# Reordering one step of a pipelined decoder: the next block's query projection between the two halves of the weighing, and FFN pieces in other places

## What is computed

```python
def attn_layer(x, Wqkv, qs, ksc, Wo):          # x: 4 x 512 x 128, 16 heads of 64
    q, k, v = split(x @ Wqkv)
    q, k = rotary(l2norm(q) * qs), rotary(l2norm(k) * ksc)
    out = local_attention(q, k, v)             # windows of 32, each looks one window back
    return out @ Wo
def ffn_layer(x, g, bln, W1, b1, W2, b2):
    xn = layernorm(x) * g + bln
    a, gate = split(xn @ W1 + b1)              # 341 + 341 columns
    return a * gelu(gate) @ W2 + b2
for i in range(6):
    x = attn_layer(shift_tokens(x), ...) + x
    x = ffn_layer(shift_tokens(x), ...) + x
```

## Time and profile before

| what | value |
|---|---|
| median of 3 runs | 2215.07 us (2211.49 to 2216.2) |
| profiled execution, its own time | 2222.9 us |
| its span, first to last instruction | 2221.1 us |
| PE matmuls busy | 2012.4 us, 91% of the span |
| DVE, ACT, POOL busy | 64%, 62%, 49% |
| mean granted PE clock | 0.983 of full speed |

### The profile page before, as it was taken

The page is one execution under the profiler, slowest core; times in us unless marked ns, Lnnn a source line. Parts: engine busy times, 40 slices in busy tenths (PEclk is TensorE's granted clock), DMA queues, the critical chain, the costliest instruction groups (busy, mean ns, idle before and its releaser), DMA issues.

```text
span 2221.1 us, 74774 instructions
## 1 busy us (share of the span) xinstructions
PE 2012.4 (91%) x32616; PEld 1183.0 (53%) x32616; DVE 1410.5 (64%) x1975; ACT 1384.2 (62%) x2029; POOL 1090.0 (49%) x709
## 2 busy tenths in 40 slices
PE   8999997789998999999999999999899998999987
PEld 5655654355555555555555555555555555555553
DVE  1454444667766776676667667766677676667753
ACT  5555554466666666766666666666666666666664
POOL 0000000576665665565656656665556555556540
PEclk9999998799999999999999999999999999999998
DMA  3000000122223222232222323222322223222220
GB/s 106 1 1 1 1 20 29 39 59 59 59 68 78 68 69 59 64 93 62 68 62 68 85 58 84 61 58 69 78 69 69 59 59 88 67 69 59 60 59 20
DMA packets 82066, 128.11 MB, mean 58 GB/s; under 512 B 17230, under 2 KB 28108, under 8 KB 81740
## 3 DMA queue, kind: packets, MB, share of 16 engines
q1 hardware_dynamic: 81740, 123.33, 21.4%
HBM read 21.55 MB, written 1.05 MB: 10 GB/s over the span
## 4 chain that ended last, share of the span: by engine, by line
PE 66%; ACT 13%; issue 11%; DVE 7%; POOL 2%; DMA 0%; ACTq 0%; POOLq 0%; DVEq 0%; SPq 0%
PE ps L617 11%; PE ps L613 11%; PE ps L639 8%; PE ps L677 7%; PE ps L670 6%; PE ps L697 4%; PE ps L426 3%; PE ps L622 3%; DVE work L1104 2%; PE ps L626 2%; ACT work L974 2%; POOL work L1421 2%; ACT work L981 2%; DVE work L1252 2%; PE ps L519 1%
## 5 line engine op out<-in xcount | busy, mean ns | idle before, releaser
L1421 POOL TENSOR_TENSOR work<-work,RS 128x1024 f32<-128x1024 f32 x192 | 365.6, 1904 | 345.8 <-ACT RS L961 342.0
L617 PEld LDWEIGHTS ps<-ident,work 128*128 128x128 f32 x3072 | 344.4, 141 | 254.5 <-issue 112.9
L617 PE MATMUL ps<-ident,work 128*128 128x128 f32 x3072 | 408.7, 276 | 68.4 <-ACT work L981 32.0
L1099 DVE TENSOR_TENSOR work<-ps,work 128x512 f32<-128x512 f32 (+1 forms) x288 | 244.6, 849 | 253.7 <-ACT work L1019 182.5
L1442 POOL TENSOR_TENSOR work<-work 128x1024 f32<-128x1024 f32 x96 | 225.8, 2352 | 149.1 <-DVE work L1104 148.9
L1427 POOL TENSOR_TENSOR work<-work,RL 128x1024 f32<-128x1024 f32 x96 | 182.8, 1904 | 141.8 <-DVE RL L1159 141.8
L1432 POOL TENSOR_TENSOR work<-work 128x1024 f32<-128x1024 f32 x96 | 226.8, 2362 | 51.0 <-DVE work L1104 51.0
L1104 DVE TENSOR_TENSOR work<-ps,work 128x512 f32<-128x512 f32 (+1 forms) x288 | 246.9, 857 | 0.0
L1144 DVE TENSOR_REDUCE SS<-work 128x16 f32<-128x1024 f32 x192 | 231.9, 1208 | 0.0
L677 PEld LDWEIGHTS ps<-work 64*32 64x32 f32 x12288 | 136.2, 105 | 166.9 <-issue 153.8
L670 PEld LDWEIGHTS ps<-KT,work 64*32 64x32 f32 x12288 | 136.6, 105 | 127.5 <-issue 125.7
(11 more groups left out here) (184 smaller groups left out, 3177.9 us busy)
## 6 DMA issues: line engine op xcount, KB each, us to landing
work<-work SPq DMA_DIRECT2D x576, 128.0 KB
work<-work SPq DMA_DIRECT2D x336, 64.0 KB
WQ<-in_wqkv SPq DMA_DIRECT2D x6, 512.0 KB, 3.6
WK<-in_wqkv SPq DMA_DIRECT2D x6, 512.0 KB, 4.1
WV<-in_wqkv SPq DMA_DIRECT2D x6, 512.0 KB, 3.5
WO<-in_wo SPq DMA_DIRECT2D x6, 512.0 KB, 3.9
work<-ZR SPq DMA_DIRECT2D x48, 64.0 KB
W<-in_w SPq DMA_DIRECT2D x6, 341.0 KB, 3.0
```

What stands on the lines that cost most here:

```text
L617: m = nc.tensor.transpose(flat(R)[:, t * 128:t * 128 + 128], src[:, t * 128:t * 128 + 128], ident[:, :])
L1099: V.tensor_tensor(h16(cos_part[:, j, cols]), h16(src), rotary_tabs[:, at:at + 64].unsqueeze(1).broadcast_to([PARTS, heads_in, 64]), ALU.mu ...
L1421: U.tensor_tensor(h16(qk_norm[:, j, :]), h16(cos_part[:, j, :]), inv_norms[:, j, :].unsqueeze(2).broadcast_to([PARTS, 16, 64]), ALU.mult). ...
```

## The change

PE: the query projection leaves the head of the step; `queries(g+1)` for the next block stands between W1 and W2, and block 0's stands before the loop. V now opens the step; Th follows it. Tk follows Th and an FFN piece. FFN pieces move: `hid(0)` before Th, `hid(1)` right behind Th, the gate of chunk 2 behind Tk, its value half behind Tq, two of the three `ffn_project` matmuls in step 1 behind S2 and the third in step 2 behind Th, three of `project_out` of step 3 behind Th, `variance` ahead of W1. ACT: squares of Q open the step, then `copy_heads` of the block weighed in the step before, then V's copy, Th's copy and the rest; the exponentials of the step's own scores stand near its end, and `invert_norms(g, 1)` last. DVE: the probability sums stand at the end of the step, `norm` ahead of `sums(1)`. POOL: the special order for step 1 goes.

PE's step after: V, [hid 0], Th, FFN piece, Tk, [gate 2], Tq, [value 2], K, S1, Tp, S2, FFN piece, W1, [project_out piece], Q of the next block, W2.

```diff
+            def queries(g):
+                pe.wait_ge(block_shifted, 2 * (g + 1))
+                pe.wait_ge(wq_loaded, 16 * (g // 16 + 1))
+                project(bank_z, w_q, 0, g % 4)
+                project(bank_z, w_q, 1, g % 4).then_inc(q_projected, 1)
...
-                if a:
-                    pe.wait_ge(block_shifted, 2 * (g + 1))
-                    pe.wait_ge(wq_loaded, 16 * (g // 16 + 1))
-                    if due(g - 2):
-                        pe.wait_ge(probs_turned_copied, g - 2)
-                    elif due(g):
-                        pe.wait_ge(q_turned_copied, g - 1)
-                    project(bank_z, w_q, 0, n)
-                    project(bank_z, w_q, 1, n).then_inc(q_projected, 1)
-                if d:
-                    pe.wait_ge(heads_copied, g - 2)
-                    turn(bank_y, heads).then_inc(heads_turned, 1)
                 if b:
                     pe.wait_ge(wv_loaded, 16 * ((g - 1) // 16 + 1))
...
+                if f is not None and n == 1:
+                    pe.wait_ge(w1_loaded, 16 * (f // 4 + 1))
+                    pe.wait_ge(ffn_input, f + 1)
+                    hid(0, bank_f)
+                if d:
+                    pe.wait_ge(heads_copied, g - 2)
+                    turn(bank_y, heads).then_inc(heads_turned, 1)
+                if f is not None and n == 0:
+                    centre(f)
+                if f is not None and n == 1:
+                    pe.wait_ge(hidden_gated, 3 * f + 1)
+                    hid(1, bank_f)
+                if f is not None and n == 2:
+                    ffn_project(f, 2, 3)
+                if fo is not None and n == 3:
+                    project_out(fo, 3, 6)
                 if b:
                     pe.wait_ge(k_normed, g)
...
+                    pe.wait_ge(gate_gelu, 3 * f + 2)
+                    hid_gate(2, bank_f)
                 if b:
                     if a:
                         pe.wait_ge(q_sin, g + 1)
...
+                if f is not None and n == 1:
+                    pe.wait_ge(hidden_gated, 3 * f + 2)
+                    hid_value(2, bank_f)
                 if a:
                     pe.wait_ge(wk_loaded, 16 * (g // 16 + 1))
...
+                if f is not None and n == 0:
+                    variance(f)
                 if f is not None and n == 1:
-                    pe.wait_ge(hidden_gated, 3 * f + 1)
-                    hid(1, bank_f)
+                    ffn_project(f, 0, 2)
...
                     weigh(0, 4)
...
+                if g + 1 < ALL_BLOCKS:
+                    if not b:
+                        pe.wait_ge(q_sin, g + 1)
+                    queries(g + 1)
                 if c:
                     weigh(4, 8).then_inc(heads_weighed, 1)
```

More of the change, by code:

```diff
@@ L751, in step @@
                     weigh(0, 4)
[L752 to L756, removed]
                 if fo is not None and n == 2:
@@ L974, in step @@
                     A(squares[:, 0, :], flat(bank_z), ACT.Square).then_inc(q_squared, 1)
+                if d:
+                    copy_heads(g - 1)
+                if f is not None and n == 1:
+                    nc.scalar.preload_act_table_set(GELU)
+                if b:
+                    act.wait_ge(values_ready, g)
+                    if due(g - 1):
+                        act.wait_ge(windows_loaded, 160 * (g - 1))
+                    A(v_rows[:, (n - 1) % 2, :], flat(bank_x), ACT.Copy).then_inc(values_copied, 1)
+                if f is not None and n == 1:
+                    gelu(f, 0, bank_f)
                 if d:
@@ L981, in step @@
                     A(heads_t[:, :, slot * 128:slot * 128 + 128], turned(bank_y), ACT.Copy).then_inc(heads_turned_copied, 1)
[L982 to L988, removed]
+                if f is not None and n == 1:
+                    gelu(f, 1, bank_f)
                 if b:
@@ L999, in step @@
                 if f is not None and n == 1:
-                    nc.scalar.preload_act_table_set(GELU)
+                    gelu(f, 2, bank_f)
                 if b:
@@ L1024, in step @@
                     A(probs_t[:, :, :], turned(bank_z), ACT.Copy).then_inc(probs_turned_copied, 1)
[L1025 to L1036, removed]
-                    inverse(f)
[L1038 to L1041, removed]
-                        copy_heads(g)
+                if f is not None and n == 0:
+                    inverse(f)
+                if b:
+                    act.wait_ge(scores_shifted, g)
+                    if due(g - 1):
+                        act.wait_ge(probs_turned, g - 1)
+                    A(probs[:, :, :, :], scores_sb[:, :, :, :], ACT.Exp).then_inc(probs_exp, 1)
+                if a:
+                    invert_norms(g, 1)
             def last_square(b):
@@ L1165, in step @@
                     rotary_cos(g, n, 0, flat(bank_z), slice(0, 1024), q_cos)
+                if f is not None and n == 1:
+                    gated(f, 0, bank_f)
+                if a:
                     if due(g):
@@ L1169, in step @@
                     sums(0, g)
+                if f is not None and n == 1:
+                    gated(f, 1, bank_f)
+                    gated(f, 2, bank_f)
                 if f is not None and n == 2:
                     update(f)
-                if f is not None and n == 1:
-                    gated(f, 0, bank_f)
                 if a:
@@ L1189, in step @@
                     V.tensor_tensor(scores_sb[:, :, :, :], by_head(bank_x), per_head(row_max[:, :]).unsqueeze(3).broadcast_to([PARTS, 8, 2, 64]), ALU.subtract).then_inc(scores_shifted, 1)
-                if f is not None and n == 1:
-                    gated(f, 1, bank_f)
+                if f is not None and n == 0:
+                    norm(f)
                 if a:
                     sums(1, g)
-                if f is not None and n == 0:
-                    norm(f)
+                if b:
+                    dve.wait_ge(probs_exp, g)
+                    V.tensor_reduce(per_head(row_sum[:, :]), probs[:, :, :, :], AX, ALU.add).then_inc(probs_sum, 1)
+                    dve.wait_ge(probs_sum, g)
+                    if due(g - 1):
+                        dve.wait_ge(probs_ready, g - 1)
+                    V.reciprocal(row_inv[:, :], row_sum[:, :]).then_inc(probs_inverse, 1)
                 if fo is not None and n == 3:
@@ L1436, in step @@
                         pool.wait_ge(block_shifted, 2 * g + 4)
-                    late = f is not None and n == 1
-                    if not late:
-                        norm_product(g, 0)
+                    norm_product(g, 0)
                     pool.wait_ge(k_cos, 2 * g + 2)
```

48 lines of the change are left out of this document (11 added, 37 removed).

## The result

The changed kernel takes **2183.96 us** (median of five runs, 2173.51 to 2189.16) against 2216.2 us for the kernel before in the same comparison (2211.49 to 2217.7): ratio **0.9861, interval 0.9841 to 0.9881**. That is 32 us less, three times the 10 us that I forecast, and inside the range of 2170 to 2242. The profiled execution of after is the fastest of the five: 2173.51 us, span 2171.7, mean granted clock 0.983. The other four have clocks of 0.975 to 0.980.

What follows compares the result with a forecast made beforehand. PE, 91% busy, was taken as the bound: 73.6 us a pass becomes 73.3 (-6 us), steps without FFN -6, tail +2, together -10: 2222.9 to 2213, or 2205 us at the median; 80% range 2170 to 2242.

Steps and rivals of the forecast that it cites:

- Instruction gaps: PE running out of instructions inside S and W: 3.0 us a pass before, 1.0 left after, W's gaps gone.
- S1, Tp, S2 is as it was, and keeps its gaps: Scores on PE: order unchanged, so S's gaps stay in steps 0, 2 and 3; part of the 1.0 us left.
- the gaps of step 0 fall into a wait anyway: Gaps in step 0 were said to cost nothing extra, falling into a wait of step 1.
- Work and waits, 71.0: PE per pass after the change: 66.7 us of work and 4.3 of waits.
- The 0.5 at Th ahead of `hid(1)`: Step 0 to 1: Th waits 0.5 us for its copy of the heads, before a 2.7 us stall at hid(1).
- The clock: Granted clock falls behind the stall at hid(1) in some 85% of passes, 1.5 us each: 1.3 us a pass, bounds 0 and 1.7.
- The eight steps without FFN: 131.6 us before, 16.4 a step; near 15.0 a step after plus 0.4 for the clock, gaining 6 us in all.
- The tail: Steps 97 and 98: hid 1 waits for gelu 0 with little beside it, costing 2 us.
- Instruction gaps stay: Rival: PE's gaps follow bytes used, not spacing, so all 3.0 us a pass remain: 2249 us; chance 0.12.
- Slower by ACT's queue: Rival: ACT's queue ahead of hid(1) in step 1 runs 1.2 us later than counted: 2231 us; chance 0.19.
- No fall: Rival: the stall at hid(1) is there but the clock holds, 29 us less: 2176 us; chance 0.17.
- the order in the text forbids it: Said against the rival that half the hid(1) stall is hidden, 64 us less: 2141 us; chance 0.07.

Runs made afterwards that it cites:

- a_both_s: Changed kernel with sums(1) ahead of norm, GELU load and gelu 0 early, and one project_out matmul between S1 and Tp in steps 2 and 3: 2111.48 us, ratio 0.9574.
- a_q_end: Changed kernel with Q of the next block behind W2 instead of between W1 and W2: 2216.38 us, ratio 1.0008 to the kernel before.
- a_norm_late: Changed kernel with sums(1) ahead of norm on DVE in step 0: 2132.18 us, ratio 0.9626 to the kernel before.
- a_gelu_first: Changed kernel with heads copy, GELU load and gelu 0 first on ACT in step 1, gated 0 ahead of the query rotation on DVE: 2128.46 us, ratio 0.962.
- a_dense: Changed kernel with Q behind W2 and the FFN pieces between S2 and W1 moved behind W1: 2289.39 us, ratio 1.0329 to the kernel before.
- b_q_mid: Kernel before with only the next block's Q moved between W1 and W2: 2314.01 us, ratio 1.0438.

## Why the prediction was right in its mechanism and wrong in its sizes

**The mechanism was right.** Each event foretold is in the trace. The gaps of W are nearly gone, a stall once a pass appears ahead of `hid(1)` behind a GELU load that follows the copy of the heads, Tk keeps a wait of 0.4, and the clock falls behind some of the stalls. Without a gap or a fall the four steps come out within 0.3 us each of what was worked out before the change was built. In step 0 to 1 of a pass without a gap, K starts at 1243.77, the inverse ends at +10.7 (11.0 worked out), squares of Q +11.6 (12.0), heads +12.6 (12.95), GELU load +13.9 (14.2), gelu 0 +15.5 (15.9), and `hid(1)` starts at +16.3 (16.65). The chain is 0.3 us shorter from its first link and otherwise to size.

**The steps that failed** are terms of the sum. The forecast of a change, 10 us, is what two nearly equal passes leave (73.6 and 73.3), and nearly every term of the second was too large. It had 71.0 of work and waits, 1.0 of gaps and 1.3 of clock: 73.3. Measured:

- *Instruction gaps, "I leave 1.0 of 3.0"*: 71.9 less 70.7 less seven falls (7 x 1.7 / 21 = 0.57) leaves about 0.65, 8 us less over 22 passes. The step that failed is "S1, Tp, S2 is as it was, and keeps its gaps": S's own gaps fell to less than half, 29.8 to 11.1 us, though nothing around S1, Tp, S2 changed. Also wrong in part is that the gaps of step 0 fall into a wait anyway. Those of W do (the step stays 21.6). One in S2 does not: in the rows above S2 resumes 1.40 us late at 1177.25, DVE's maximum starts 6.2 us behind K instead of the 5.0 of the pass without a gap, and the step takes 22.9 instead of 21.6, for S2 feeds DVE's queue to `sums(1)`, the same chain.

```profile
1177.99 1.22 DVE L1177 TENSOR_REDUCE MX<-ps 128x16 f32<-128x1024 f32 x1 [1.10 <-PE ps L678]
```

- *Work and waits, 71.0*: 70.7. The 0.5 at Th ahead of `hid(1)` is not there (1256.40, no wait); as the chain is 0.3 shorter, the copy of the heads ends when PE arrives. 7 us less over 22 passes.
- *The clock, "with some 85% of passes and 1.5 us each"*: a fall costs the 1.7 us of the upper bound, but comes in a third of the passes (profiled) to some 60% (median run, an estimate from its clock), 0.55 to 1.1 us a pass instead of 1.3. At the median run 5 us less.
- *The eight steps without FFN*: 124.5 us instead of 131.6, 7 less where the prediction had 6. That is luck in part. Its own terms (11.4, 1.04, 1.1, 1.74) add up to 15.3 and not to "near 15.0", which would make it 4, and 4.6 of the 7 us lie in two of the eight steps.
- *The tail*: "+2" for `hid(1)` waiting at the end did not come. From the K of step 92 to the end it is 137.7 before and 135.4 after; a pass's own 1.7 taken off, 0.7 less.

The prediction's 4.3 us a pass of waits before is a remainder (7.3 less 3.0); the rows that it names for them print 53.3 us in 21 passes, 2.5 a pass, and waits of about 0.6 at W1 for DVE's rotation, in 13 of the passes, belong to it too.

**Adding up.** At the medians the change is 32 us instead of 10, 22 more. The terms above give 8 + 7 + 5 + 1 + 3 = 24 of them. Between the two profiled executions the difference is 49: 35 in 21 passes (73.56 and 71.91), 7 in the eight steps, 2 behind them, and 5.5 ahead of the first K, which starts at 401.6 us instead of 407.1. Those 5.5 are not the change's. Of the 14 profiled executions of this study twelve, three kernels built on the one before among them, have their first K at 401.6 to 403.7 us; only before (407.1) and `a_both_s` (406.9) start it later, and why they do stays open. So most of the 7.8 us by which the profiled execution of before lay above its median stood ahead of the pipeline, and the prediction was right to take them off. The profiled execution of after lay 10.5 below its own median, with about seven falls fewer.

**The rivals.** "Instruction gaps stay" fell with `a_q_end`: same bytes, other spacing, gaps back. "Slower by ACT's queue" did not come true, but its price did: `a_norm_late` and `a_gelu_first` take 1.4 and 1.6 us off that step and gain 52 and 54 us, more than 22 for each us, as the clock holds too. "No fall" is half true. The Trainium skill (TensorE: Matmul & The Clock Gate, section Why this matters for your kernels) warns only of idle gaps longer than these, and the trace differs from it: seven falls stand behind stalls of 2.3 to 2.6 us, and 15 stalls of 2.1 to 2.6 passed at full clock. The length of the stall alone doesn't decide, and what does stays open.

**Where the gain went.** Fewer gaps are worth some 45 to 50 us (40 gaps fewer, 1.0 us printed and up to 0.25 more each). The old waits at W1, Tk and Tq were worth what the new ones are: the shortest steps of before sum to 17.0 + 20.4 + 17.7 + 15.5 = 70.6 us, after's to 70.7. The clock takes 12 to 24 us back. This split is read from the steps of two traces; `a_q_end` brings W's gaps back only together with a wait, so no run prices them alone. The prediction left open that the stall could be removed without giving up the rest; "the order in the text forbids it" holds of that text only, and two small moves gave 73 us more.

## What to carry to other kernels

A large matmul that moves takes its cover with it: list, for each place it leaves, which copy on another engine ran beneath it, before you price what it gains at its new place. Here parts of the change, put into the kernel before, cost 98, 129 and 107 us, while the whole of it, with V ahead of Th, a piece between Th and Tk, and the exponentials off the head, gained 32. Once a change has turned several short waits into one long one, follow that one back through the engines' queues: the longest chain was ACT's and DVE's order ahead of one matmul, and reordering it gave more than the change itself.

## What the runs showed of the hardware

**PE runs out of instructions where small matmuls are dense.** In the kernel before, PE resumed behind the 66 gaps inside S and W 1.25 to 1.55 us (10th to 90th percentile, median 1.41) after the end of a packet of the instruction queue; from random moments the last packet's end lies 3.8 us back. The same holds after (26 gaps, median 1.40), and in `a_q_end` (46, 1.36), `a_dense` (60, 1.40) and `b_q_mid` (32, 1.40). One of them: packet from 1205.83 to 1207.16, PE resumes at 1208.56. The 258 packets are the same in all; what differs, as I read it, is whether PE has used up what it holds when the next arrives. With 512-column matmuls between the dense groups 58.7 us of gaps became 18.7, and half of those in S went too although only W was spread, which I read as PE drawing less in all from its stock; that reading was not tested by itself.

**The clock can fall behind a stall of 2.3 to 2.6 us**, for 1.7 us each time, in a number of passes that differs from run to run (0.983 to 0.974). Over ten runs of the changed kernel the time follows the clock (correlation -0.95) over a spread of 17 us; with the stall shortened the spread is 3 to 5.
